# Retention block with an FP4 feed-forward: the decayed queries move from VectorE to GpSimd, and the weights' rounding steps move behind the scores

## The reference, cut to what matters

```
q, k, v = split(x @ w_qkv.T);  q, k = xpos(q, k)            # rotary, scaled
out[t]  = sum over s <= t of (q[t] . k[s]) * scale * decay^(t-s) * v[s]     # per head
y       = (silu(x @ w_gated.T) * norm(out)) @ w_proj.T
x       = layernorm(x + y)
```

```
x = layernorm(x + fp4(silu(fp4(x) @ fp4(w_gate).T) * (fp4(x) @ fp4(w_up).T)) @ fp4(w_down).T)
```

## Time and profile before

| | before |
|---|---|
| median of 3 runs | 651.88 us |
| the profiled execution, its own time | 651.12 us |
| its span | 649.3 us |
| TensorE matmuls, busy | 583.6 us, 90% |
| VectorE, busy | 552.7 us, 85% |
| ScalarE, busy | 337.6 us, 52% |
| GpSimd, busy | 230.9 us, 36% |
| mean granted TensorE clock | 0.964 |

### The profile page before, as it was taken

One profiled execution on the slowest core, in us unless ns is written; L12 is line 12 of the kernel. 1 busy time (PEld: TensorE's weight loads), 2 busy tenths in 40 slices (PEclk: granted clock), 3 DMA queues, 4 the chain that ended last, 5 costly groups with the idle time before them and its releaser, 6 DMA issues. The chain is left out here.

```text
span 649.3 us, 14685 instructions
## 1 busy us (share of the span) xinstructions
PE 583.6 (90%) x4290; PEld 498.6 (77%) x4290; DVE 552.7 (85%) x1439; ACT 337.6 (52%) x869; POOL 230.9 (36%) x262
## 2 busy tenths in 40 slices
PE   3269999999999999999999967786999999999975
PEld 2158888888888888888888856676999888888864
DVE  6047779999999999999999767887999999999996
ACT  3124666666756675667565654423454435444333
POOL 1011122344234523452344023435444444444430
PEclk9679999999999999999999979797999999999998
DMA  6471011101110111011101000000000000000001
GB/s 160 56 231 49 11 50 50 40 8 48 48 40 8 48 48 40 8 48 48 40 8 40 11 8 9 1 1 17 16 16 16 16 16 24 24 16 16 17 16 50
DMA packets 25853, 23.11 MB, mean 36 GB/s; under 512 B 2024, under 2 KB 22760, under 8 KB 25832
## 3 DMA queue, kind: packets, MB, share of 16 engines
q1 hardware_dynamic: 25016, 21.27, 11.6%
q10 hardware_dynamic: 816, 1.57, 0.7%
HBM read 17.56 MB, written 5.28 MB: 35 GB/s over the span
## 5 line engine op out<-in xcount | busy, mean ns | idle before, releaser
L1178 PE MATMUL wide_banks<-win_hi,x_hi 128*128 128x512 f32 x192 | 68.8, 440 | 12.9 <-DVE win_lo L882 11.0
L1154 POOL TENSOR_TENSOR shared<-shared,h_scale 128x704 f32<-128x704 bf16 x32 | 44.4, 1388 | 92.0 <-DVE shared L802 92.0
L1178 PE MATMUL wide_banks<-wgu_hi,xq_hi 128*128 128x512 f32 (+1 forms) x192 | 63.4, 413 | 10.6 <-DVE xq_lo L979 10.6
L442 ACT ACTIVATE shared<-opened,rstd 128x64 f32<-128x64 f32 x256 | 64.7, 335 | 11.4 <-DVE rstd L715 11.1
L413 ACT ACTIVATE shared<-shared 128x704 bf16<-128x704 f32 x32 | 25.3, 792 | 81.0 <-POOL shared L1149 81.0
L1237 PEld LDWEIGHTS mixed<-shared 128*128 128x128 f32 x512 | 62.0, 192 | 2.8
L1100 POOL TENSOR_TENSOR kd<-shared 128x128 f32<-128x128 f32 x60 | 23.2, 407 | 111.1 <-DVE shared L610 87.8
L1149 POOL TENSOR_TENSOR shared<-shared,h_inv 128x704 f32<-128x704 f32 x32 | 44.5, 1391 | 50.7 <-DVE h_inv L793 50.7
L1178 PE MATMUL wide_banks<-win_lo,x_hi 128*128 128x512 f32 x192 | 61.3, 401 | 0.0
L1178 PE MATMUL wide_banks<-win_hi,x_lo 128*128 128x512 f32 x192 | 60.9, 398 | 0.0
L1237 PE MATMUL mixed<-shared 128*128 128x64 f32 x512 | 60.6, 271 | 0.0
(11 more groups left out here) (147 smaller groups left out, 1487.8 us busy)
## 6 DMA issues: line engine op xcount, KB each, us to landing
xf<-in_x_feat SPq DMA_DIRECT2D x32, 128.0 KB, 2.3
tab<-in_tables SPq DMA_DIRECT2D x16, 256.0 KB, 2.7
xt<-in_x_tok SPq DMA_DIRECT2D x32, 128.0 KB, 2.1
out<-shared SPq DMA_DIRECT2D x32, 128.0 KB, 1.7
x<-in_w_in ACTq DMA_DIRECT2D x3, 512.0 KB, 5.3
w<-in_w_gu SPq DMA_DIRECT2D x1, 1408.0 KB, 7.7
pow_dram<-powers SPq DMA_DIRECT2D x1, 1056.0 KB
w<-in_w_down SPq DMA_DIRECT2D x1, 704.0 KB, 9.0
```

The costliest lines, as they stand in the source:

```text
L442: last = act.activation(gated[:, b, cols], opened[:, b, cols], ACT.Copy, scale=rstd[:, b, 1 + k:2 + k])
L1154: pool.tensor_tensor(over_blocks(hq[:, b]), over_blocks(h_steps[:, b]), spread(h_fp4["scale"][:, b]), ALU.mult).then_inc(h_fp4["ready"], 1)
L1178: last = pe.matmul(dst, lhs, rhs, start=k == 0, stop=k == len(parts) - 1)
```

## The change: what it does

It moves `decay_q` from VectorE to GpSimd, between `decay_k` and `split_x`. There it reads ScalarE's copy `qkT` in SBUF instead of the PSUM bank `turn`. The transposition of the gated heads accordingly waits for that copy (`qkT_ready`) and no longer for the decayed queries. On VectorE `decay_scores` now comes ahead of `w_unit` and `w_exponent`, and on ScalarE `copy_gatedT` comes ahead of `round_w_from`.

```
 ScalarE body
+                if in_turn(n - LAG):
+                    copy_gatedT(n - LAG)
                 if piece is not None and b == 1:
                     round_w_from(piece)
-                if in_turn(n - LAG):
-                    copy_gatedT(n - LAG)
...
 VectorE
-            def decay_q(n):
-                dve.wait_ge(qkT_ready, n + 1)
-                if isinstance(n, int) and n == 0:
-                    dve.wait_ge(ld_mask, 16 * (GROUPS + PER))
-                need(dve, out_done, n)
-                dve.tensor_tensor(qdT[:].rearrange("p g t -> p (g t)"), turn[:, 0:GROUPS * P],
-                                  dq[:].rearrange("p g t -> p (g t)"), ALU.mult).then_inc(qd_ready, 1)
...
 VectorE body
-                if valid(n):
-                    decay_q(n)
                 if joint:
                     joint_square(n)
                     joint_product(n)
                     joint_fine(n)
                     joint_fine_square(n)
+                if valid(n):
+                    decay_scores(n)
                 if w and b == 1:
                     w_unit(piece)
                     w_exponent(piece)
-                if valid(n):
-                    decay_scores(n)
...
 GpSimd
+            def decay_q(n):
+
+                pool.wait_ge(qkT_ready, n + 1)
+                need(pool, out_done, n)
+                pool.tensor_tensor(qdT[:], qkT[:, 0:GROUPS], dq[:], ALU.mult).then_inc(qd_ready, 1)
...
 GpSimd body
                 if carried(n):
                     decay_k(n, b)
+                if valid(n):
+                    decay_q(n)
                 if valid(n + 2) and not (isinstance(n, int) and n < 0):
                     split_x(n + 2, b)
...
 TensorE turn_gated
-                    pe.wait_ge(qd_ready, n + LAG + 1)
+                    pe.wait_ge(qkT_ready, n + LAG + 1)
```

## The result

| | before | after |
|---|---|---|
| median | 651.63 us (4 runs) | 663.26 us (4 runs, 662.25 to 664.37) |
| ratio, after over before | | 1.018, 95% interval 1.0155 to 1.0205 |
| profiled execution, its span | 651.12, 649.3 us | 662.85, 660.7 us |

The change makes the kernel 11.6 us slower; 664 was forecast. The stretch view of the loop, first of the kernel after, answers to the earlier trace rows. The stretch is 10.4 us longer and holds a little less work (it ends 1.8 us ahead of tile 30's masked scores, the one before 0.4 us ahead). TensorE is as busy as before (255.9 us), so what was added is waiting; VectorE is shown busy 10 us more although an instruction a tile was taken from it, because an instruction that is held counts as busy, and GpSimd 17 us more.

What follows compares the result with a forecast made beforehand. Bound: a ring per tile pair between VectorE's masked scores and TensorE, both engines nearly full. A + B = 22.6 against 21.6, +12 over 12 pairs, +0.5 outside: +12.5 on 651.88, so 664 us; range 648 to 670.

Steps and rivals of the forecast that it cites:

- A: Loop time from even masked scores to the odd ones: 11.19 us before, forecast 10.6 (10.36 to 10.87).
- B: Loop time from odd masked scores to the next even ones: 10.44 us before, forecast 12.0 (11.92 to 12.13).
- The first hold: Even to odd scores: GpSimd's new product holds VectorE's L735 until 215.52, 0.50 us later, with nothing lost.
- the near tie: Even to odd scores: weights' scales at 215.77, 0.05 us behind split_x, too close to call; 10.36 to 10.87, middle 10.6.
- The second hold: Even to odd scores: split_x holds the remaining weights' scales until 216.31, bringing VectorE's path to 10.87 us.
- TensorE's floor of 10.36: Even to odd scores: the least time, set by TensorE's scores ending at 216.32 and L625 about 0.05 us later.
- The ladder: Odd to next even scores: VectorE's chain L675 to L700 meets decay_q and split_x one after the other, held to 10.66 and 11.4.
- The fork at L675: Odd to next even scores: L675 gets through, masked scores at 11.92 us, or is held to 9.98, scores at 12.13.
- the third rival: Loop: ScalarE's late pass has unseen slack and TensorE sets the pace; 6 us faster, 646; chance 0.04.
- Not held: Loop: the new GpSimd instruction does not hold VectorE; pair 21.26 us, 4 us faster, 648; chance 0.16.
- One hold only: Odd to next even scores: decay_q slips in and the chain meets split_x alone; +3 us, 655; chance 0.13.
- ScalarE's pass costs nothing: Same as the third rival: the chain behind ScalarE's late pass has slack; 646 us; chance 0.04.

Runs made afterwards that it cites:

- the order alone: Kernel before with masked scores ahead of w_unit and w_exponent and copy_gatedT ahead of round_w_from, decayed queries left on VectorE: 654.30 us, 1.004.
- The run with the pass behind the state: Kernel after with ScalarE's pass over the weights (round_w_from) put behind place_state: 659.42 us, 1.012 to the kernel before.
- the windows kernels: Kernel before with GpSimd's weight steps behind x_exponent, x's rounding in the next even tile: 651.43 us; plus reordering 645.81; plus decay_q on GpSimd 648.30.

## Why the prediction was right

**The sum.** It gave A 10.6, B 12.0, a pair 1.0 us longer and +12.5 us; measured were A 10.65, B 11.98, +1.01 and +11.6. The 12 pairs account for the change: from the masked scores of tile 6 to those of tile 30 it is 259.2 us before and 270.9 after. The +0.5 outside the loop was not there: what precedes tile 6 moved by 0.1, what follows tile 30 by -0.4. One slip of arithmetic did no harm: the upper bound, 23.0 against 21.63, gives +16.4, not +17.

**Part A.** GpSimd's product lasts 0.73 as taken from `split_x`, begins 0.07 after the copy, and does not delay `split_x`. The first hold was as worked out. On the near tie the truth lay in between the bounds, but by another road than a mean, so that 10.65 for 10.6 is partly luck. The second hold came: the first scale of the weights (220.93) got through 0.02 us ahead of `split_x`, the second was held. That is nearly the upper bound of 10.87. It came out 0.22 lower because `split_x` starts 9.56 us behind the even scores, not 9.71 as before, and because one scale fewer was held. TensorE's floor of 10.36 was too high as well, since late even scores shorten A on TensorE's side: the order alone reached 10.20. The difference of A between it and the kernel after is 0.45.

**Part B.** The ladder came step by step: keys' decays, `decay_q`, `split_x` back to back, and L675, L679, L685 held by one each (forecast 9.98, 10.66 and 11.4 for the ends of the holds; taking the ends less 0.18 from the rows above, 9.80, 10.49 and 11.17, all 0.2 early because the whole of B was). The fork at L675 went the way of the upper bound, 12.13 forecast for it; that the 12.0 written down was met to 0.02 is luck, since the fork cost 0.13 more than the middle and everything came 0.15 to 0.2 early. By the Trainium skill (VectorE: DVE Perf Modes, "What auto-detection actually checks") a step like L675, one source and an even outer dimension, uses both ports. The trace agrees in so far as the step was held: 0.37 us for 0.18 in the kernel after, 0.35 in the order-only one. By the Trainium skill (SBUF — State Buffer, "Who interferes with whom") a VectorE instruction with two inputs in SBUF and a GpSimd one that reads SBUF exclude each other for the whole instruction. The trace agrees with the exclusion, and on its end differs by 0.15 us, as L694 did by 0.14: L677, with both inputs in SBUF, ends 0.03 us after the recorded end of `split_x`, with 0.18 of its own to run.

**The step that was off.** "L642 starts at 7.42", given to ScalarE's late pass, measured 7.27. ScalarE was late as said, but it was hardly later than VectorE. These rows of the kernel after lie behind the odd masked scores at 222.04:

```profile
224.10 0.50 ACT L409 ACTIVATE w_rounder<-w_rounder 128x352 f32<-128x352 f32 x1 [1.34 <-DVE w_rounder L770]
...
227.71 0.62 ACT L404 ACTIVATE x_rounder<-x_rounder 128x512 f32<-128x512 f32 x1
...
228.46 1.29 POOL L1104 TENSOR_TENSOR x_unit<-x_unit,x_rounder 128x512 f32<-128x512 f32 x1 [0.54 <-ACT x_rounder L404]
...
228.70 0.58 ACT L434 ACTIVATE squares<-mixed 128x512 f32<-128x512 f32 x1
...
228.87 0.41 DVE L610 TENSOR_TENSOR shared<-qk_cos,wide_banks 128x256 f32<-128x256 f32 x1
...
229.31 0.69 DVE L634 TENSOR_TENSOR opened<-mixed,shared 128x512 f32<-128x512 f32 x1
```

L409 starts at 2.06 (2.14 forecast); the squares and the rotation both end at 229.28, 7.24 (7.42 forecast for the squares). The prediction had not worked out VectorE's own path in B, which `w_unit`, `w_exponent` and longer holds on `x_unit` (1.20 for 1.08) and `x_exponent` (0.97 for 0.82) lengthen nearly as much. Its sign for the third rival, whether L642 follows the rotation or the squares, is a near tie for that reason. The run with the pass behind the state shows what ScalarE's pass was worth: 0.1 us on `apply_gate`, and 0.37 on L404 and the GpSimd queue behind it, which is what B ends with. The prediction had that queue, and ScalarE did end last on it. But of the 1.55 us by which B grew, only 0.37 hang on ScalarE's pass: without it B is still 11.61, by VectorE's path and the GpSimd queue behind it. So the account of ScalarE waiting for L409 explains the last 0.37 and leaves out what would have taken its place.

**The rivals.** *Not held*: false by every row above. The prediction's third instance, L735 in the feed-forward, had only the next GpSimd row beside it. The one that held it is this, of the kernel before; it ends at 438.95, L735 at 438.99.

```profile
437.56 1.39 POOL L1154 TENSOR_TENSOR shared<-shared,h_scale 128x704 f32<-128x704 bf16 x1 [2.45 <-DVE shared L802]
```

*One hold only*: the chain met two new ones and the keys' decays. *ScalarE's pass costs nothing*: false, since moving it away gains 3.8 us. Of the move and the reordering neither alone gives the change: +9.5 and +3.0 us by the medians, which add up to about the 11.6 of both. Why they add up so nearly was not tested.

## What to carry to other kernels

Before work goes from VectorE to GpSimd, list what VectorE does in SBUF alone at that time, how long GpSimd's instructions stand back to back there, and what depends on the last of VectorE's tiny steps: each step of a dependent chain can wait for one whole GpSimd instruction. Ask of a freed engine whether it was the one that ended last; here VectorE had more busy time after it was relieved. When a path turns out late, ask which other path ends just ahead of it: taking ScalarE's wait away gave 0.37 us a pair, and then VectorE's queue stood in its place. And look for the pauses of the second engine that the kernel already uses: the pause of 1.0 us behind the keys' decays was where the chain ran.

## What the runs showed of the hardware that was not expected

**GpSimd is held as well.** In the windows kernels, where the three weight steps meet no `x_unit`, they take 0.94, 0.95 and 0.79 us. In the kernel before, the third starts while `x_unit` runs and takes 1.01. In the kernel after it is the second: it starts at 203.06, while `x_unit` (from 202.34, held itself until the first weight step ended) runs to 203.54, and takes 1.26; the third is back at 0.79. The longer one is always the one that begins under `x_unit`.

**A few hundredths decide 12 us.** Two kernels that differ only in a spare instruction of 0.61 or 0.73 us are 11 us apart, mostly because 12 pairs of tiles repeat the same near misses (0.52 us in A, 0.22 in B; in the profiled executions 8.6 us of the difference lie in these pairs and 1.6 ahead of them): a step at 0.05 us ahead of `split_x` takes 0.17, one at 0.06 us behind takes 0.70.

**A waiting VectorE step goes first.** Between two GpSimd instructions back to back, one VectorE step is let in each time (209.39, 210.08, 210.76 above), and the next dependent one, 0.2 us later, is behind again. So a chain of tiny steps that has fallen behind goes forward by one step for each GpSimd instruction, and is free only when the run of them ends.
